# Cross-attention and quantised FFN on one core: scores with queries on partitions, transposes by DMA, a new order of the side work

## The reference

```
ln(x)   = (x - mean) / sqrt(var + 1e-5)                        # over 1024 columns
hidden  = concat([context, ln(x)], axis=1)                     # 64 + 512 rows
q = (ln(x) @ Wq.T) -> 16 heads x 96;   k, v = hidden @ Wk.T, hidden @ Wv.T -> 4 heads x 96
attn    = softmax(q k^T / sqrt(96));   x = x + (attn v) @ Wo.T
fq(t)   = clip(round(t / s), -128, 127) * s,  s = max(|t|) / 127 by row
x       = x + fq(silu(fq(ln(x)) @ fq(Wgate).T) * (fq(ln(x)) @ fq(Wup).T)) @ fq(Wdown).T
```

## Time and profile before

| | us |
|---|---|
| median of the three timed runs | 1901.45 |
| the profiled execution, its own time | 1894.81 |
| its span, first to last instruction | 1893.1 |
| TensorE busy | 1801.7 |
| VectorE busy | 1247.4 |
| ScalarE busy | 688.1 |
| GpSimd busy | 22.1 |

### The profile page before, as it was taken

One profiled execution on the slowest core, in us unless ns is written; L12 is line 12 of the kernel. 1 busy time (PEld: TensorE's weight loads), 2 busy tenths in 40 slices (PEclk: granted clock), 3 DMA queues, 4 the chain that ended last, 5 costly groups with the idle time before them and its releaser, 6 DMA issues. The chain is left out here.

```text
span 1893.1 us, 25912 instructions
## 1 busy us (share of the span) xinstructions
PE 1801.7 (95%) x8588; PEld 825.5 (44%) x8588; DVE 1247.4 (66%) x2056; ACT 688.1 (36%) x996; POOL 22.1 (1%) x45
## 2 busy tenths in 40 slices
PE   5999999999999999999999999999968999999997
PEld 2634444454344445444444544444433444444443
DVE  6546577544657754465775446577548989899894
ACT  3245457214545721464572146457221111111110
POOL 0000000000000000000000000000000000000000
PEclk9999999999999999999999999999988999999999
DMA  4023353212435321243532124353384342433422
GB/s 183 23 85 127 113 174 120 78 52 71 142 112 170 115 81 59 70 143 113 165 121 80 59 70 142 113 172 116 139 308 118 92 108 60 102 91 77 102 71 75
DMA packets 131842, 208.90 MB, mean 110 GB/s; under 512 B 85776, under 2 KB 85840, under 8 KB 126608
## 3 DMA queue, kind: packets, MB, share of 16 engines
q1 hardware_dynamic: 68416, 188.77, 30.0%
q10 hardware_dynamic: 62592, 15.80, 4.6%
q0 software_dynamic: 720, 2.88, 0.4%
HBM read 157.29 MB, written 34.21 MB: 101 GB/s over the span
## 5 line engine op out<-in xcount | busy, mean ns | idle before, releaser
L564 PE MATMUL ps_o<-p_sb,v_sb 128*97 128x512 f32 (+1 forms) x640 | 317.1, 607 | 0.0
L1148 PE MATMUL ps_gu<-w_gu_sb,xT 128*128 128x512 bf16 (+1 forms) x1152 | 231.8, 361 | 1.1 <-DVE g_sb L1283 1.0
L1189 ACT ACTIVATE g_sb<-g_sb,sx 128x512 f32<-128x512 f32 (+1 forms) x128 | 73.1, 581 | 393.5 <-DVE g_sb L1283 306.6
L851 DVE TENSOR_REDUCE mx_parts<-ps_g 128x1 f32<-128x512 f32 x256 | 165.8, 683 | 22.3 <-PE ps_g L527 21.1
L843 DVE SCALAR_TENSOR_TENSOR q_lo<-ps_g,q_hi 96x512 f16<-96x512 f32 x102 | 70.3, 690 | 158.9 <-ACT q_hi L650 158.1
L697 ACT ACTIVATE p_sb<-ps_s 128x512 f32<-128x512 f32 (+1 forms) x320 | 172.6, 596 | 6.0 <-PE ps_s L553 3.8
L913 DVE SCALAR_TENSOR_TENSOR x_acc<-ps_g,x_acc 128x512 f32<-128x512 f32 x128 | 87.0, 690 | 125.9 <-PE ps_g L482 119.2
L1161 PE MATMUL ps_d<-w_dn_sb,hT 128*128 128x512 bf16 x704 | 160.9, 382 | 7.1 <-DMA hT<-h_int 7.1
L1148 PEld LDWEIGHTS ps_gu<-w_gu_sb,xT 128*128 128x128 bf16 x1152 | 112.0, 98 | 118.3 <-DVE g_sb L1283 5.9
L480 PE MATMUL ps_g<-xnT_hi,wq_hi 128*128 128x512 f16 x408 | 155.4, 381 | 1.4 <-DVE xnT_lo L801 1.4
L481 PE MATMUL ps_g<-xnT_lo,wq_hi 128*128 128x512 f16 x408 | 155.1, 380 | 0.0
(11 more groups left out here) (118 smaller groups left out, 2523.8 us busy)
## 6 DMA issues: line engine op xcount, KB each, us to landing
w_in<-wqT SPq DMA_DIRECT2D x18, 1536.0 KB, 7.5
w_in<-w_gu SPq DMA_DIRECT2D x40, 512.0 KB, 4.1
w_in<-woT SPq DMA_DIRECT2D x12, 1536.0 KB, 6.6
inv_sum<-inv_d SPq DMA_DIRECT2D x64, 192.0 KB, 3.3
gu_q<-w_t SPq DMA_DIRECT2D x44, 256.0 KB, 7.4
w_in<-w_dn SPq DMA_DIRECT2D x8, 1376.0 KB, 7.1
w_gu_sb<-gu_q SPq DMA_DIRECT2D x3, 2816.0 KB, 13.9
x_acc<-x SPq DMA_DIRECT2D x4, 2048.0 KB, 9.1
```

The source lines that it names most:

```text
L564: mm = nc.tensor.matmul(ps_o[0:HD + 1, :], v_sb[0:rows, t, kv, :], p_sb[0:rows, j % 2, t, :], start=(t == 0), stop=(t == ST - 1))
L851: nc.vector.tensor_reduce(mx_parts[:, t, g, 0:1], bank(b, u)[:], AX.X, ALU.max).then_inc(mx_red, 1)
L1148: mm = nc.tensor.matmul(ps_gu[n % NR][:, 0:nu * P], xT[:, k, :], w[:, u0:u0 + nu, k, :], start=(k == 0), stop=(k == KD - 1))
```

## The change

Scores are now made with the queries on partitions: for each of the 16 heads of a batch there are 4 tiles of 128 queries by 576 keys, three matmuls of 512 and three of 64 columns each, into a PSUM tile of two banks (`ps_s` is 2 x [128, 1024] instead of 4 x [128, 512]). VectorE takes the negated row maximum of the finished tile, and ScalarE uses it as the bias of the exponential. ScalarE makes the exponential twice: in float32 with the row sum as accumulated output, and in float16. GpSimd subtracts the two to a float16 low part. High and low part of a tile, 1152 columns, are transposed by one DMA. The coarse maxima, their transposes and their DMA are gone, and so is the float32 product with the values: that is now 14 float16 matmuls a head. The last 64 keys have high and low part stacked on 128 partitions. Weights and tokens are transposed by DMA too. All transposes are issued by SyncE, in the FFN as well.

```
-            mm = nc.tensor.matmul(ps_o[0:HD + 1, :], v_sb[0:rows, t, kv, :], p_sb[0:rows, j % 2, t, :], ...)
+        def score_tile(b, j, t):                       # TensorE
+            pe.wait_ge(p_done, head_tile(b, j, t) + 1)
+            for i, (l, r) in enumerate(((qh, k_hi), (qh, k_lo), (ql, k_hi))):
+                nc.tensor.matmul(o[:, 0:T], l, r[0:HD, kv, 0:T], start=(i == 0), stop=(i == 2))
+                mm = nc.tensor.matmul(o[:, T:S], l, r[0:HD, kv, T:S], start=(i == 0), stop=(i == 2))
+        def pv_tile(b, j, t):                          # TensorE; for t == 0 it waits for o_mul and all p_turned
+            nc.tensor.matmul(o, v_lo[:, t, kv, :], p[:, t, :], start=(t == 0), stop=False)
+            mm = nc.tensor.matmul(o, v_hi[:, t, kv, :], p[:, t, :], start=False, stop=(t == TT))
+            if t < TT:
+                nc.tensor.matmul(o, v_hi[:, t, kv, :], p[:, ST + t, :], start=False, stop=False)
+        def row_max(b, j, t):                          # VectorE
+            dve.wait_ge(s_done, head_tile(b, j, t) + 1)
+            nc.vector.tensor_reduce(neg_max[:, j % 2, t:t + 1], scores(j, t), AX.X, ALU.max, negate=True)
+        def chances(b, j, t):                          # ScalarE; waits for mx_done, p_low, p_turned
+            nc.scalar.activation(p_f[:, t % NF, :], s, ACT.Exp, bias=bias, accum_out=sums[:, j % 2, t:t + 1])
+            nc.scalar.activation(p_nat[:, t % NN, 0:S], s, ACT.Exp, bias=bias).then_inc(p_done, 1)
+        def chances_lo(b, j, t):                       # GpSimd
+            nc.gpsimd.tensor_tensor(n[:, S + C:2 * S], f[:, 0:T], n[:, 0:T], ALU.subtract)
+            nc.gpsimd.tensor_tensor(n[:, S:S + C], f[:, T:S], n[:, T:S], ALU.subtract)
+        def turn_chances(b, j, t):                     # SyncE
+            sp.wait_ge(p_low, head_tile(b, j, t) + NF + 1)
+            sp.dma_start_transpose(pT[:, j % 2, :, t * P:(t + 1) * P], p_nat[:, t % NN, :])
```

```
+    units = {0: v[:2], 1: v[2:], 2: q[1][:1], 3: q[1][1:], 4: q[2][:1], 5: q[2][1:2], 6: q[2][2:] + o[0][:2],
+             7: o[0][2:6], 8: o[0][6:] + q[3][:1], 9: q[3][1:], 10: o[1][:2], 11: o[1][2:4], 12: o[1][4:6],
+             13: o[1][6:], 14: q[0][:1], 15: q[0][1:]}          # 16: o[2];  17: KEYS + o[3]
+COST = {"V": 24 * 162 / 2, "Q": 24 * 217 / 2, "K": 24 * 125 / 2, "WO": 9 * 217}
+STAGED = [[("w", 0)], [("w", 1)], [("w", 2)], [("q", 1, 2), ("w", 3)], [("q", 2, 0), ("q", 2, 1)],
+          [("q", 2, 2), ("o", 0)], [("q", 3, 0), ("w", 4)], [("q", 3, 1), ("w", 5)], [("w", 6)],
+          [("q", 3, 2), ("o", 1)], [("q", 0, 0), ("w", 7)], [("q", 0, 1), ("w", 8)], [("w", 9)], [("w", 10)],
+          [("oh", 2, 0), ("oh", 2, 1)], [("q", 0, 2), ("w", 11)], [("q", 1, 0), ("q", 1, 1)], [("o", 3), ("w", 12)]]
+LN_STEPS = (9, 10, 11, 12)
+            def batch(b):                              # SyncE
+                for j in range(STEPS):
+                    if 1 <= j <= H:
+                        turn_chances(b, j - 1, 2)
+                        turn_chances(b, j - 1, 3)
+                        inverses_out(b, j - 1)
+                    if u is not None:
+                        turn_weights(b, u, turns(u)[0])
+                    if j < H:
+                        turn_chances(b, j, 0)
+                    if j - 1 in LN_STEPS and not last:
+                        turn_tokens(b, LN_STEPS.index(j - 1))
+                    if j < H:
+                        turn_chances(b, j, 1)
+                    if u is not None:
+                        store_weights(b, u, turns(u)[0])
...
+                    for n in range(2, NW):
+                        if free_step(n - 2) == j:
+                            load_stage(b, n)           # waits until item n - 2 is out of its buffer
+                    if 1 <= j <= H:
+                        inverses_in(b, j - 1)
```

More of the change, by code:

```diff
@@ new lines, in pieces, with step_order @@
+def pieces(u):
+    parts = 1 if u[0] == "WO" else 2
+    return [("X", u, i, parts) for i in range(parts)]
+COST = {"V": 24 * 162 / 2, "Q": 24 * 217 / 2, "K": 24 * 125 / 2, "WO": 9 * 217}
+def step_order(j, last):
+    others = [("PV", j - 2, t) for t in range(ST)] if j >= 2 else []
+    others += [p for u in side_work(j, last) for p in pieces(u)]
+    cost = [COST[o[1][0]] if o[0] == "X" else (3 if o[2] < TT else 2) * 217 for o in others]
+    before = sum(c for o, c in zip(others, cost) if j <= H or o[0] == "PV" or o[1][0] != "WO")
+    total, done, order, k = before, 0, [], 0
+    for o, c in zip(others + [None], cost + [0]):
+        while k < 4 and (o is None or done >= total * k / 4):
+            order += ([("S", j, k)] if j < H else []) + [("mark", k)]
+            k += 1
+        if o is not None:
+            order.append(o)
+            done += c
+    return order
@@ new lines, in turns, with units_of @@
+def turns(u):
+    return [u] if u < GU else [GU + 2 * (u - GU), GU + 2 * (u - GU) + 1]
+def units_of(last):
+    return [a[1] for j in range(STEPS) for a in step_order(j, last) if a[0] == "X" and a[2] == 0]
+STAGED = [[("w", 0)], [("w", 1)], [("w", 2)], [("q", 1, 2), ("w", 3)], [("q", 2, 0), ("q", 2, 1)],
[3 rows of a table added]
+STAGE = [s for step in STAGED for s in step]
+STAGE_STEP = [j for j, step in enumerate(STAGED) for _ in step]
+UNIT_STEPS = [j for j, step in enumerate(STAGED) for s in step if s[0] == "w"]
@@ L479, in three @@
+            def three(o, pairs, first, last):
                 for i, (l_hi, l_lo, r_hi, r_lo) in enumerate(pairs):
-                    nc.tensor.matmul(o, l_hi, r_hi, start=(i == 0), stop=False)
+                    nc.tensor.matmul(o, l_hi, r_hi, start=(first and i == 0), stop=False)
                     nc.tensor.matmul(o, l_hi, r_lo, start=False, stop=False)
-                    mm = nc.tensor.matmul(o, l_lo, r_hi, start=False, stop=(i == len(pairs) - 1))
-                return mm
-            def transposes(b, t, h):
-                if h == 0:
-                    pe.wait_ge(ln_y, tile_no(b, t) + 1)
-                o = claim(b, ("T", t, h))
-                for i in range(4):
-                    c = (4 * h + i) * P
-                    mm = nc.tensor.transpose(o[:, i * P:(i + 1) * P], token_tile(b, t)[:, c:c + P], ident[:])
-                mm.then_inc(g_done, 1)
@@ new lines, in batch @@
+            def batch(b):
+                for j in range(STEPS):
+                    for kind, *a in step_order(j, is_last(b)):
+                        if kind == "S":
+                            chances(b, *a)
+                        elif kind == "X" and a[1] == a[2] - 1 and a[0][0] in step:
+                            step[a[0][0]](b, *a[0][1:])
+                        elif kind == "mark":
+                            mark(b, j, *a)
+            act.wait_ge(dconsts, 3)
+            act.sem_inc(p_done, 2)
@@ new lines, in _ @@
+            tokens_hi(None, 0)
+            tokens_hi(None, 1)
+            w_split(wq_hi[:], None, 0)
+            tokens_hi(None, 2)
+            context_hi(1)
+            tokens_hi(None, 3)
+            w_split(wk_hi, None, 1)
+            for u in PRO:
+                step[u[0]](None, *u[1:])
+                for after, hi, n in pro_splits(wq_hi, wv_hi):
+                    if after == u:
+                        w_split(hi, None, n)
+            with act.Fori(0, B - 1) as b:
+                batch(b)
@@ L790, in _ @@
+            batch(B - 1)
         @block.vector
@@ L995, in ffn_phase @@
+                for (after, hi, n), (_, lo, _) in zip(pro_splits(wq_hi, wv_hi), pro_splits(wq_lo, wv_lo)):
+                    if after == u:
+                        w_split(hi, lo, None, n)
+            with dve.Fori(0, B - 1) as b:
+                batch(b)
+            batch(B - 1)
 def ffn_phase(nc, x2, gu_q, dn_q, kept, out):
```

1118 lines of the change are left out of this document (549 added, 569 removed).

## The result

The changed kernel takes 1885.94 us (median of 8 runs, 1875.28 to 1894.99); the kernel before took 1900.37 us beside it. The ratio is 0.9927, 95% interval 0.9906 to 0.9947: 0.7% faster. I had forecast 1759 us with a range of 1650 to 1870. The sign was right, and nearly all of the forecast gain (142 us) did not come.

The account below looks back on a forecast made before the run. The prediction took TensorE to set the attention phase's pace, with DMA late next and the fullest engine setting each step. Span 65 + 3 x 297 + 275 + 520 = 1751 us, timed 1759, range 1650 to 1870.

Parts of the forecast that it names:

- The count of matmuls: TensorE in a batch: 311 us of matmuls less 51.4 removed by the change, leaving 260 us.
- the prologue: Before the first batch: tokens pass ScalarE, GpSimd and a DMA before the first Q; batches start at 65 instead of 47.4 us.
- The step that failed: Allowance for new waits in a batch: 5%, 14 us on 283, half a step of slack hiding most; 297 us a batch.
- The batch's edge: Step 0 of a batch was costed as set by TensorE, at 10.9 us.
- VectorE's fullest step: Within a batch, VectorE was to set step 5 and step 9 (16.8 us); step 10 had VectorE 11.9 under DMA 15.6.
- DMA: In a batch: 120 us of transposes, 1.4 us per 1152-column tile, plus 107 other traffic; 227 us of 260, setting some steps.
- Rival (c): DMA transposes do not overlap in their queue, 3.3 us per 1152 columns: 387 us a batch, timed 2115; chance 0.11.
- The clock: TensorE's granted clock falling in the gaps was listed as a sign the prediction was wrong, with no size.
- (b): SyncE's single list leaves 2 us bare in each of 18 steps: 319 us a batch, timed 1849; chance 0.17.
- (a): TensorE sets every step, transposes overlapping near their lower bound: 278 us a batch, timed 1679; chance 0.21.
- The last batch: Fourth batch, without K and three Q units: 253 x 1.05 = 265, plus 10 before the last WO: 275 us.
- GpSimd beside VectorE: Shared port blocking VectorE's two-port modes: up to 20 us a batch on VectorE, 4 showing, +16 us in all.

Follow-up runs that it names:

- e11: Changed kernel with transposes of 128 columns, staged loads of 64, first two staging loads ahead of the stores, exponentials not waiting for row maxima; results invalid: 1709.53 us.
- after: The changed kernel itself, as profiled after the change, against the kernel before: 1885.94 us, ratio 0.9927.
- e7: Changed kernel with constant exponential bias, so ScalarE waits for scores alone; VectorE reduces a constant tile instead, same amount of work: 1819.87 us, 0.9577 of the kernel before.
- e5: Changed kernel with the next batch's first two weight tiles loaded before the stores at a batch's end: 1859.3 us, 0.9783 of the kernel before.
- e6: Changed kernel with next batch's first two weight loads ahead of the stores and the residual's load moved from step 2 to step 4; nothing left out: 1846.63 us.
- e9: Changed kernel with 80 idle 512-column matmuls a batch added on TensorE just before measured waits: 1882.84 us, 0.9907 of the kernel before.
- e2: Changed kernel with every staged weight load moving 64 columns instead of 1024 to 3072, instructions keeping their sizes: 1819.93 us, 0.9575 of the kernel before.
- e3: Changed kernel with both head-tile transposes cut to 128 columns and staged weight loads cut to 64: 1809.47 us, 0.952 of the kernel before.
- e1: Changed kernel with each DMA transpose of a head tile moving 128 columns instead of 1152: 1851.36 us, 0.974 of the kernel before.

## Why the prediction was wrong, by its own steps

**Right.** The count of matmuls (260 us; e11's 264 busy at clock 0.99), the prologue (67.5 for 65), the end (520.3 for 520), VectorE (207 for 200); GpSimd is 15% over (117 for 102). ScalarE (168 for 175) is luck: its exponentials with the sum's output take 107 us a batch where I had 96, and what is left beside them 61 where I had 79. These are from after's groups by form, as in the earlier trace rows:

```profile
L550 POOL TENSOR_TENSOR p_nat<-p_f,p_nat 128x512 f16<-128x512 f32 x256 | 317.7, 1241 | 808.0 <-ACT p_nat L798 807.6
L928 DVE TENSOR_REDUCE small<-ps_s 128x1 f32<-128x576 f32 x256 | 191.6, 750 | 91.1 <-PE ps_s L677 89.0
L796 ACT ACTIVATE p_f<-ps_s,small 128x576 f32<-128x576 f32 x256 | 189.6, 741 | 455.2 <-DVE small L928 426.2 <-DVE small L934 28.9
L798 ACT ACTIVATE p_nat<-ps_s,small 128x576 f16<-128x576 f32 x256 | 187.9, 734 | 0.8 <-DMA pT<-p_nat 0.8
...
L551 POOL TENSOR_TENSOR p_nat<-p_f,p_nat 128x64 f16<-128x64 f32 x256 | 111.9, 437 | 0.0
```

A pair on GpSimd is 1.24 + 0.44 = 1.68 us on average (taken: 1.6, the middle between two bounds far apart, so luck as well); the row maximum is 0.75 as taken. An exponential is 0.74 rather than 0.65, and the sum's output 0.195 (taken: 0.2).

**The step that failed.** "Half a step of slack hides most, since a score tile waits only for the exponentials two tiles earlier ... I take 5% (before it was 7%), 14 us: 297 a batch." The mechanism stood in the text: second staging buffer, VectorE in front of the row maxima, ScalarE behind those, TensorE behind both. Only its size was taken from the share of stalls before, when the exponentials did not wait for VectorE at all. Measured, the term is 334.9 - 283 = 52 us a batch above the steps' maxima, not 14; counted from the 260 us of matmuls it is 75 (51 idle, 24 slowed) where 37 were forecast. e7 shows that the round itself is 66 us of the run, e5 that the batch's edge is 27, e6 that the residual's load is 13.

**The batch's edge was not in the sum.** Step 0 was costed as TensorE 10.9 us. I had not listed what SyncE issues between two batches: transposes, two 1 MB stores and two stores of weights, and only then the loads for which the first VectorE work waits. It takes 24.4 us with an 11.0 us wait.

**VectorE's fullest step was misplaced.** `STAGED` names the output weights in steps 5 and 9, the two steps of the first ten that I let VectorE set. In the trace VectorE comes to them 1 to 2 us into steps 6 and 10 (at 494.64 and 562.22). So it has 10.0 us in step 9 where I had 16.8, and 18.2 in step 10 where I had 11.9 and let the DMA set the step at 15.6.

**DMA.** 227 us forecast, 268 measured; 1.67 to 1.93 us a transpose instead of 1.4. Traffic beside them explains 1.67 to 1.93 at most; why even the lower figure is above my upper bound of 1.59 is open. Shares of 1.03 to 1.05 came with lengths near the forecast in steps 11 and 13, and with 2.0 and 4.4 us more in steps 12 and 14. Rival (c) is out: steps 11 and 13 hold four transposes of chances, one of weights and one of tokens each, 4 x 3.3 + 3.1 + 3.8 = 20.1 us by (c), and last 15.9 and 12.3 us. The transposes do overlap.

**The clock** was named as something that would make the prediction wrong, without a price. It costs up to 24 us a batch here, and it is not a cause of its own: it comes with the stops and goes with them (e11). Fillers raised it and gained no time (e9).

**The rivals.** (b) gave 319 a batch and 1849 us by a latency in each of 18 steps. The total is nearest to it, but not the mechanism: the excess sits mostly in six places. In steps 0 and 3 it is one late load, in steps 6 and 10 no load is late and VectorE's own work fills most of the step; the others were not followed up. (a) is not reached even by e11 (1709.5 for 1679).

**The last batch**: 312.4 for 275. Its final wait, for the low part of head 15 (L960), is 12.7 us where I had added 10; the rest is the same excess as in the others.

**GpSimd beside VectorE.** The Trainium skill's rule that VectorE's two-port modes and GpSimd block each other (Advanced Engine Details and Errata, section VectorE Performance Modes) was weighed at +16 us for the run, and not put into the sum. The mean of VectorE's low part of 3072 columns hides it (3355 ns before, 3438 after). Single instructions show it. First each engine alone (the rounding of a weight tile on VectorE, the 64-column subtraction on GpSimd), then both at once, twice:

```profile
430.16 0.68 DVE L986 TENSOR_SCALAR w_int<-w_in 128x1024 bf16<-128x1024 f32 x1
428.07 0.31 POOL L551 TENSOR_TENSOR p_nat<-p_f,p_nat 128x64 f16<-128x64 f32 x1
...
581.47 1.28 DVE L986 TENSOR_SCALAR w_int<-w_in 128x1024 bf16<-128x1024 f32 x1
582.17 0.75 POOL L551 TENSOR_TENSOR p_nat<-p_f,p_nat 128x64 f16<-128x64 f32 x1
...
494.64 3.36 DVE L873 SCALAR_TENSOR_TENSOR wo_lo<-w_in,wo_hi 128x3072 f16<-128x3072 f32 x1
494.67 3.49 POOL L551 TENSOR_TENSOR p_nat<-p_f,p_nat 128x64 f16<-128x64 f32 x1
```

Behind the start of VectorE's low part GpSimd's subtraction of 0.31 us takes 3.49: it stands still until VectorE is done. So the trace shows the blocking that the rule states, though whether that low part runs in a two-port mode no row shows. It is part of GpSimd's 117 us for 102. What it costs the run was not tested.

**Open.** What separates e6 (1847 us, nothing left out) from e11 (1710 us, much left out) is mainly the link (some 66 us) and the DMA time (some 76). A third score tile or a third staging buffer would separate them in a whole kernel; neither was tried. How much of e2's 66 us is bytes and how much the latency of each load is not told apart.

## What to carry to other kernels

When work is taken from the bound engine, price the wait chain that is left, not only the fullest engine of each step: list, for every queue that is worked off in order, and above all for the loads' queue across the loop's edge, what stands ahead of the item that the next engine waits for. Do not carry over the stall share of the old kernel when the change adds an engine to the round through a double buffer: here VectorE was busy 62% of the time and its place in the round cost 66 us. Before a long instruction is cut up, look at what ends the wait behind it; if the engine would have waited anyway, it was free.

## What the runs showed of the hardware that was not expected

- Behind the stop of 3.13 us that ends at 457.78, TensorE's matmuls start 0.40 to 0.43 us apart instead of 0.21, the level of 1.2 GHz, until 460.69; the mean granted clock over a batch is 0.92, where it was 1.00 before.
- A transpose of a 128x1152 float16 tile by DMA costs 1.67 us of all 16 engines beside short loads (e2 against e3) and 1.93 beside full loads (after against e1): 295 KB, so 177 and 153 GB/s. The earlier trace rows showed 186 to 246 for transposes in the FFN.
- A two-operand subtraction on GpSimd has a median of 1157 ns for 512 columns and 306 for 64: 1.9 ns a column, with some 180 ns fixed. The means of 1241 and 437 hold the stops beside VectorE.
- VectorE and GpSimd stopped each other in some pairs of instructions: a rounding on VectorE of 0.68 us took 1.28, a GpSimd subtraction of 0.31 us took 3.49 beside a VectorE low part of 3072 columns. VectorE's row maximum out of PSUM stayed at 0.75 us beside the same subtractions.
